# Rotating q in two parts, and another order of the first products, in a fused perceiver block

## What is computed

```python
x = x + cross_attention(layernorm(x), ctx)     # 32 batches, 32 queries of 512, 257 keys
x = x + causal_self_attention(layernorm(x))
x = x + expert_ffn(layernorm(x))               # top 2 of 8 experts

# cross_attention, 16 heads of 32:
q = x @ Wq + bq;  k, v = split(ctx @ Wkv + bkv)
q, k = rotate(q), rotate(k)    # te*cos - to*sin, te*sin + to*cos on even/odd columns
out = softmax(q @ k.T / 8) @ v @ Wo + bo
```

## Time and profile before

| | |
|---|---|
| median of 3 runs | 796.67 us (796.67, 792.99, 796.69) |
| the profiled execution, its own time | 795.88 us |
| its span in the trace | 794.1 us |
| TensorE busy | 756.5 us, 95% of the span |
| VectorE / ScalarE / GpSimd busy | 493.9 / 418.6 / 326.6 us |
| mean granted TensorE clock | 0.98 |
| DMA | 77.96 MB, mean 98 GB/s |

### The profile page before, as it was taken

How to read it: one execution, slowest core, us unless ns; L and a number is a source line. 1 busy time by engine, 2 the same in 40 slices (tenths; PEclk the granted TensorE clock), 3 DMA queues, 4 the chain that set the end, 5 groups by cost and what they waited for, 6 DMA issues and landing times. The chain is left out here.

```text
span 794.1 us, 23428 instructions
## 1 busy us (share of the span) xinstructions
PE 756.5 (95%) x9650; PEld 667.8 (84%) x9651; DVE 493.9 (62%) x1209; ACT 418.6 (53%) x978; POOL 326.6 (41%) x366
## 2 busy tenths in 40 slices
PE   8999999999999999999999999999899999689997
PEld 7998899989989989998898998998577777568884
DVE  5776655555566565556556556666789998822236
ACT  5464656455565555655555555665556674123330
POOL 0654355444444535635443553442123321146640
PEclk9999999999999999999999999999999999879999
DMA  8414100111010111011101011021663227635538
GB/s 303 189 31 158 36 30 28 47 44 29 29 35 29 55 35 30 29 35 52 33 28 35 29 54 30 5 105 56 268 250 138 116 94 300 240 122 167 186 132 317
DMA packets 23175, 77.96 MB, mean 98 GB/s; under 512 B 3329, under 2 KB 4737, under 8 KB 20129
## 3 DMA queue, kind: packets, MB, share of 16 engines
q1 hardware_dynamic: 19392, 64.45, 22.9%
q0 software_dynamic: 3680, 12.06, 4.6%
HBM read 57.89 MB, written 18.61 MB: 96 GB/s over the span
## 5 line engine op out<-in xcount | busy, mean ns | idle before, releaser
L164 PE MATMUL bank<-chi,wparts 128*128 128x258 f32 x496 | 143.4, 289 | 0.5 <-DVE v L757 0.5
L166 PE MATMUL bank<-chi,wparts 128*128 128x258 f32 x496 | 140.1, 282 | 0.0
L165 PE MATMUL bank<-clo,wparts 128*128 128x258 f32 x496 | 139.9, 282 | 0.0
L392 POOL TENSOR_TENSOR ksin<-kb,const 128x516 f32<-128x516 f32 x64 | 89.7, 1402 | 109.7 <-ACT kb L505 109.7
L412 POOL TENSOR_TENSOR ctx_sums<-craw 128x512 f32<-128x512 f32 x30 | 39.5, 1315 | 147.1 <-DVE ctx_sums_lo L774 147.1
L505 ACT ACTIVATE kb<-bank,bias_cols 128x258 f32<-128x258 f32 x126 | 60.0, 476 | 66.4 <-PE bank L166 66.4
L164 PEld LDWEIGHTS bank<-chi,wparts 128*128 128x128 f32 x496 | 94.0, 189 | 1.1 <-DVE v L757 0.7
L165 PEld LDWEIGHTS bank<-clo,wparts 128*128 128x128 f32 x496 | 94.3, 190 | 0.0
L166 PEld LDWEIGHTS bank<-chi,wparts 128*128 128x128 f32 x496 | 94.0, 189 | 0.0
L746 DVE TENSOR_TENSOR kcos<-kb,const 128x516 f32<-128x516 f32 x64 | 53.8, 842 | 23.1 <-ACT kb L505 23.1
L510 ACT ACTIVATE pr<-pr,nmax 128x257 f32<-128x257 f32 x128 | 63.5, 500 | 5.8 <-DVE nmax L782 5.8
(11 more groups left out here) (380 smaller groups left out, 2236.0 us busy)
## 6 DMA issues: line engine op xcount, KB each, us to landing
craw<-ctx_t_dram SPq DMA_DIRECT2D x32, 516.0 KB, 3.6
expert_lo<-weights_dram SPq DMA_DIRECT2D x8, 1024.0 KB, 13.0
expert_hi_scratch<-wraw SPq DMA_DIRECT2D x16, 512.0 KB, 2.7
wparts<-expert_hi_scratch SPq DMA_DIRECT2D x8, 1024.0 KB, 10.0
wraw<-weights_dram SPq DMA_DIRECT2D x7, 1024.0 KB, 5.5
expert_lo<-ffn_out_scratch SPq DMA_DIRECT2D x16, 256.0 KB, 5.6
x<-x_dram SPq DMA_DIRECT2D x8, 256.0 KB, 7.6
ffn_xn_scratch<-xn SPq DMA_DIRECT2D x8, 256.0 KB, 2.4
```

The costliest lines, as they stand in the source:

```text
L164: pe.matmul(psum, ahi(c), bhi(c), start=(c == 0), stop=False)
L165: pe.matmul(psum, ahi(c), blo(c), start=False, stop=False)
L166: last = pe.matmul(psum, alo(c), bhi(c), start=False, stop=(c == chunks - 1))
L392: pool.tensor_tensor(ksin[:, part, :], kb[:, part, :], sink[:, part, :], ALU.mult).then_inc(s_ksin, 1)
```

## The change

- In `body(t)` of VectorE, `q_rope` is cut into `q_trig` (the two products with cosines and sines) and `q_rotate` (the four combinations). At j = 3 `q_trig(t + 1)` now stands between `o_sum` and `inverse_sums`, and `q_rotate(t + 1)` between `pair_parts` and `o_lo`. Before, both stood after `ctx_lo`.
- At the start, TensorE transposes the first tile inside `first_k_product`, ahead of its fourth and last chunk, and the two `warm_up` products behind it are gone.
- At the start, ScalarE copies K of batch 0 out ahead of rounding the V weights, VectorE makes `kcos` ahead of their low parts and puts `q_bias(0)` between the second and the third of these, and SyncE loads cosines and sines ahead of the V weights.
- GpSimd makes `ksin` of batch 0 ahead of the copy of `same`.

```diff
                 weight(WQ)
+                sp.dma_start(const[:, C_COSK:C_ALL], const_in[:, C_COSK:C_ALL]).then_inc(s_const, 16)
                 weight(WV)
-                sp.dma_start(const[:, C_COSK:C_ALL], const_in[:, C_COSK:C_ALL]).then_inc(s_const, 16)
...
                 pool.wait_ge(s_const, 16)
-                pool.tensor_copy(same[:], const[:, C_SAME:C_SAME + P]).then_inc(s_same, 1)
                 k_sin(0, 0)
                 k_sin(0, 1)
+                pool.tensor_copy(same[:], const[:, C_SAME:C_SAME + P]).then_inc(s_same, 1)
...
                 w_hi_chunks(WQ, range(2, KC))
-                wv_plain()
                 for m in range(4):
                     k_evac(0, m)
+                wv_plain()
...
-                def q_rope(t):
+                def q_trig(t):
                     dve.wait_ge(s_qb, t + 1)
                     qv = qb[:].rearrange("p (a i) -> p a i", i=16)
                     dve.tensor_tensor(xn[:].rearrange("p (a i) -> p a i", i=16), qv, cosq, ALU.mult)
                     dve.tensor_tensor(qsin[:].rearrange("p (a i) -> p a i", i=16), qv, sinq,
                                       ALU.mult).then_inc(s_qcos, 1)
+
+                def q_rotate(t):
                     dve.wait_ge(s_qcos, t + 1)
...
                 w_lo_chunks(WQ, range(2, KC))
-                wv_plain_lo()
-                dve.wait_ge(s_bq, 16)
                 dve.wait_ge(s_const, 16)
-                q_bias(0)
-                q_rope(0)
                 k_cos(0, 0)
                 k_cos(0, 1)
+                wv_plain_lo(0)
+                wv_plain_lo(1)
+                dve.wait_ge(s_bq, 16)
+                q_bias(0)
+                wv_plain_lo(2)
+                wv_plain_lo(3)
+                q_trig(0)
+                q_rotate(0)
                 ctx_lo(1, 1)
...
                             o_sum(b - 1)
+                        if j == 3 and not last:
+                            q_trig(t + 1)
                         inverse_sums(b)
                         pair_parts(b)
+                        if j == 3 and not last:
+                            q_rotate(t + 1)
...
-                        if j == 3 and not last:
-                            q_rope(t + 1)
...
                     for c in range(KC):
                         pe.wait_ge(s_wklo, c + 1)
+                        if c == KC - 1:
+                            pe.wait_ge(s_ident, 16)
+                            xn_transposed(0)
...
                 first_k_product()
-                pe.wait_ge(s_ident, 16)
-                xn_transposed(0)
-                warm_up(quad[:, 3, :], 2)
                 q_product(0)
```

More of the change, by code:

```diff
@@ L839, in v_last, with wv_plain_lo @@
                     dve.tensor_tensor(vlast[:], sums[:, :, 1, :], vlast[:], ALU.add).then_inc(s_last, 1)
-                def wv_plain_lo():
-                    for n, (dst, raw) in enumerate(((wv_block(F_11), wv_raw(0, 0)), (wv_block(F_12), wv_raw(1, 0)),
-                                                    (wv_21, wv_raw(0, 1)), (wv_block(F_22), wv_raw(1, 1)))):
-                        dve.wait_ge(s_wkhi, WV_PARTS + n + 1)
-                        dve.tensor_tensor(dst[1], raw, dst[0].bitcast(F32), ALU.subtract).then_inc(s_wklo, 1)
+                def wv_plain_lo(n):
+                    dst, raw = ((wv_block(F_11), wv_raw(0, 0)), (wv_block(F_12), wv_raw(1, 0)),
+                                (wv_21, wv_raw(0, 1)), (wv_block(F_22), wv_raw(1, 1)))[n]
+                    dve.wait_ge(s_wkhi, WV_PARTS + n + 1)
+                    dve.tensor_tensor(dst[1], raw, dst[0].bitcast(F32), ALU.subtract).then_inc(s_wklo, 1)
                 def wv_sums_lo():
```

## The result

The changed kernel takes **784.16 us** (median of 4 runs, 782.47 to 785.27) against 796.68 us (4 runs, 792.99 to 798.40): ratio 0.985 with a 95% interval of 0.981 to 0.989, that is 9 to 15 us less. The profiled execution took 784.54 us, its span is 782.7 us. The prediction was 786.1 us. One execution of this study, of the kernel with the transposes inside the first K product, took 1,031.48 us at a mean granted clock of 0.65, and is in none of the times and ratios that follow.

What follows compares the result with a forecast made beforehand. TensorE, busy 95% of the span, was taken as the bound, its largest wait being for q's rotation. From the profiled 795.88 us: 6.9 less (last steps), 3.7 less (clock), 0.8 more (start), giving 786.1 us; range 778.5 to 791.5.

Steps and rivals of the forecast that it cites:

- the step's term: Last steps of tiles: v_22 ready sooner, 0.99 us gained per tile, 6.9 us in seven; bounds 0 and 13.0 us.
- The walk through the last step: Timing of VectorE and GpSimd from 84.44: q's stall goes, ksin precedes second kcos, v_22 at 94.42, new stall 0.9 us.
- two diagonals alternate with the first two combinations, to 89.4: In a tile's last step, GpSimd's diagonals (0.6 us each) and VectorE's combinations (0.34 us each) take turns at the port.
- The clock term: Behind the old stalls: granted-clock drops vanish with shorter stalls, 3.7 us gained; bounds 0 and 3.7.
- The start: At the start: q product at 14.83 instead of 16.27, yet VectorE's chain to the rotation ends 0.8 us later.
- the first rival: Last steps: VectorE reaches second kcos before GpSimd asks, total 780.0 us; chance 0.25.
- the start's good bound: At the start: -1.4 us, if VectorE loses nothing.
- the second with its bad one: Clock drops stay, total 789.8 us, chance 0.17; taken with the start at +2.0 us, its stall costing clock too.
- All of the stall goes: Last steps: VectorE reaches second kcos 0.35 us sooner than walked, before GpSimd asks; 13.0 us gained, 780.0 us; chance 0.25.
- The stall only moves: Last steps: v_22 comes no earlier; 0 to 2 us gained, half the clock, about 795 us; chance 0.06.
- The clock doesn't come back: Drops are tied to attend and scores, or new stalls bring them too; 789.8 us; chance 0.17.
- The context loads become late: Loads behind clo take 6.6 us, not 3.6; ScalarE waits 1.9 us in seven tiles; 803.1 us; chance 0.02.

Runs made afterwards that it cites:

- the filled stall ahead of v_fourth: Three constant matmuls between diagonals_spread and v_fourth, added to the old-start kernel with both parts of q's rotation behind pair_parts: 791.64 us, against 797.13 us unfilled.
- the start alone: The kernel before with only the new start, q_trig and q_rotate together where q_rope stood: 791.62 us, ratio 1.0015.
- The kernel with the added wait: The changed kernel, but in last steps of tiles GpSimd's second ksin waits for VectorE's second kcos, so kcos goes first: 775.35 us, ratio 0.980.

## Why the prediction came out right

784.16 us lies in the range and 1.9 us under the forecast. The mechanism was right, and the nearness of the number is in part luck: the step's term was 2.3 us too small and the clock's, between medians, some 2.4 too large. On the second chip the change brought 9.8 us, which is about what the terms as measured add up to (9.2 and 1.3 less, 1.2 more); of the 12.5 us between the medians of the first comparison some 3 stay unexplained. By its own steps:

- **The walk through the last step** named the right events: no wait before the transposes, ksin ahead of the second kcos, this kcos over 1.5 us long (1.68), a new wait for v_22. Its size was off. The walk had v_22 at 94.42, it was there at about 94.0; so a step gained 1.32 us and not 0.99, and the tiles 9.2 us and not 6.9. The error is in "two diagonals alternate with the first two combinations, to 89.4": VectorE got its first combination (87.56, 0.41 us) in at once, and the rotation ended at 89.75 and not 90.1. Behind that, every event stands 0.3 to 0.4 us ahead of its forecast, and their distances are as forecast (clo's end 91.7 for 92.0, ksin's 92.8 for 93.15).
- **The clock term** of 3.7 us was there in the profile (3.70 us over before, 0.54 after; no 4-us window after has less than 0.97 of the clock between the first scores and the end of the cross attention). But it was the size of one execution, and a bad one: the profiled execution before had a mean clock of 0.980, while 70 runs of the same kernel on four chips have 0.978 to 0.991 and 0.9855 in the mean. The changed kernel's nine runs have 0.987 in the mean. That is 1.3 us of 790; the sum should have carried the term at a third. The mechanism is shown by the filled stall ahead of v_fourth. For the old stall, ahead of the transposes, there are only the counts: a drop behind 5 of 14 when idle, behind 0 of 7 when filled.
- **The start** was forecast 0.8 us later and came 1.3 us later in the profile. The times agree (q product 14.83 forecast and 14.68 measured, first V product 20 and 19.71, rotation's end 25.3 and 24.8), but they were worked out from a profile whose start was late by chance. Against the other old starts (q's transposes at 23.65 to 23.96) the changed kernel's are 1.0 to 1.3 us late without the drop of the clock, and 1.9 to 2.3 with it in the first profile; first scores are at 27.4 to 28.3 with the new start and 26.1 to 26.4 with the old one. The term that was mis-sized is the 1.44 us by which VectorE's chain starts sooner: with TensorE's part of the new start alone, the q product came 0.9 us sooner (14.54 for 15.42). In the time of whole runs the start's price isn't clear of the scatter (the start alone: -0.3 to +2.7 us).
- **What was not in the sum**: -1.3 us by the first step (in part tied to the start, as said above) and +1.6 us behind the cross attention, chance of these executions, which nearly cancel.
- **The range** isn't the sum that it is said to be: the first rival with the start's good bound is 777.8, the second with its bad one 791.0, where 778.5 to 791.5 is stated. The result lies in both.

The rivals. *All of the stall goes* asked that VectorE reach the second kcos before GpSimd; it missed by 0.09 us. The kernel with the added wait is this rival made true: 7 x 0.8 us less, and its last step is 2.14 us shorter than before, more than the 1.86 it was priced at. *The stall only moves* needed other edits: with both parts behind `pair_parts` it is what happens, and there it was dearer than priced, because the moved stall takes clock. *The clock doesn't come back* is excluded by the windows of this trace, and that shorter stalls would bring drops too by 0 of 35 in the table, though between medians only 1.3 of the 3.7 us came back. *The context loads become late* did not happen: 3.4 us to landing.

The Trainium skill's rule of the port (SBUF — State Buffer, Terms, shared port pair: whoever starts first holds the pair for the whole instruction) agrees with these traces, with 1.11 us for an operation on 128x8 that takes 0.17 alone. By it a gap of VectorE is free only where GpSimd is idle too. The traces agree: the first gap met only the end of ctx_sums and 0.4 us of o_bias, and the two products lost 0.36 and 0.20 us in it; the second met ksin and both diagonals and was worth 0.1 us per tile.

## What to carry to other kernels

Moving work into a gap pays only if the operation that TensorE waits for next comes sooner; write down that operation's time before and after, and not the gap's width. A gap in which the other side of the port is at work is hardly a gap: what the idle time gives, the waits at the port take back. Where VectorE and GpSimd share a port and ask within a tenth of a microsecond of one another, one added wait on a semaphore can fix the order (it was worth 0.8 us per tile here, more than half of what the change itself gave). Read the clock, and the times of a start too, from many executions before they enter a sum. Where TensorE must idle for a microsecond or two, matmuls on constants may be cheaper than idling: they gave 4 us at one place and nothing at the other.

## What the runs showed of the hardware

- An idle time of TensorE of 1.7 us, ahead of the transposes of q or of a V product, is followed by a drop of the granted clock to 1.2 GHz for some microseconds in about a third of cases (10 of 28); filled with matmuls, in none of 14. Moved from ahead of the transposes of q to ahead of v_fourth, the same 1.7 us cost more: mean clock 0.980 against 0.9865 on one chip, 0.981 against 0.984 on another. The traces don't show where, with a drop behind 5 of 14 stalls at either place.
- At the port, a small operation waits as long as a large one: the pair's last part, 128x8, took 1.11 us beside a ksin instead of 0.17, half of kcos 1.68 instead of 0.68. Waiting sides got their turns alternately: two combinations of 0.83 us between diagonals of 0.87 and 0.79.
- The sums into v, with one input in PSUM, did not lose to the port: 0.41 us beside a ksin at 92.54 in the kernel with kcos first, and 0.41 to 0.43 us for all 90 of these sums in the trace after, 75 of which run beside an operation of GpSimd.
- TensorE pauses for "issue" (idle with nothing that the profile shows to wait for) once or twice in the cross attention of some executions, 0.4 to 1.1 us at a time. The place isn't chance: seven traces have a pause of over 0.4 us, and in six of them it stands in the 27th step, 2.0 to 2.6 us behind its first scores. In the seventh, of the kernel with the constant matmuls in the old stall, the pauses stand at 196 and 363 us. What does it stays open. So does the drop of the clock in the first step.
